# A feed-forward stage with silu moved to ScalarE and its down product in half-precision pairs

## The chip, the cores and the metric

The kernel runs on one core of one Trainium2 chip. The metric is device time in microseconds (us) of one execution; several executions are summed up by their median. Four compute engines work side by side and meet only at semaphores: TensorE (PE, matrix products; PEld is its loading of weights), VectorE (DVE), ScalarE (ACT) and GpSimd (POOL). SyncE (SP) issues the transfers. SBUF is the on-chip memory, PSUM the banks into which TensorE writes.

## The reference, cut to what matters

A block of a network over x of 8 x 256 tokens x 256 features: a modulated layer norm, a gated delta-rule attention (16 key heads, 32 value heads), a residual, and a second modulated layer norm with a sparse feed-forward. The change lies in the feed-forward:

```python
h = silu(einsum('bsh,hi->bsi', x, w_gate)) * einsum('bsh,hi->bsi', x, w_up)   # 256 -> 1024
h_sparse = sparsify_2to4(h)      # of each 4 neighbours the 2 largest in magnitude stay
y = einsum('bsi,ih->bsh', h_sparse, w_down)                                     # 1024 -> 256
x = x + gb * y                   # gb: gate of the sequence, at least 0.25 in magnitude
```

silu(g) is g * sigmoid(g), which equals g * (tanh(g / 2) + 1) / 2. Everything is asked for in float32.

## The kernel before

One program holds all the work. A long loop of 64 steps (16 heads x 4 pairs of sequences) computes the attention and takes some 1,900 us. Around 1,925 us `last_bodies` drains it, while the weights of the feed-forward are loaded and split. Then 16 units follow (`for u in range(UNITS)` on each engine), and these are what the change touches. The order of each engine's instructions is written out by hand; engines wait for one another by semaphores (`need(engine, name, count)`).

A unit u is one half (512) of the 1,024 features for a pair of token tiles, as four planes, so that the four neighbours of a group lie in four planes at the same place. It has 128 partitions x 1,024 values. The steps of a unit:

- PE: `gate(u)` and `up(u)`, 24 half-precision products each. Weights and activations are each held as a high and a low half-precision part, and three products (high x high, high x low, low x high) stand for one float32 product. `gate` writes bank 2 to 5 (two banks for even, two for odd units), `up` banks 6 and 7.
- ACT: `gate_tanh(u)`, two halves of 512, into `cc` (`f_th`, L1304); `magnitude(u)`, the absolute values of 1,024 (L1310).
- DVE: `silu(u)`, (tanh + 1) times the gate bank, two halves of 512 (L1751, into `b_le`); `hidden_product(u)`, times the up bank (L1762, into `e_b` for even and `kn` for odd units); `compare` (L1770 to L1772) and `count` (L1776 to L1782) rank the four planes; `select(u)` keeps two of four (L1793) and writes one of four float32 buffers (`o`, `osq`, `zth`, `zg`).
- PE: `down(j)`, the down product of token tile j, from the two units of its pair: float32 features times float32 weights `wd_sb` (the tile `ae`).
- DVE: `gate_down(j)` (L1800) multiplies by the sequence's gate; POOL: `add_residual(j)` (L481) adds x; SP stores the tile.

Beside this the layer norm of later token tiles runs: DVE `gated` (L1727), `hidden_normed` (L1742), `hidden_stats` (L1733, L1735); POOL `add_input` (L464), `hidden_rstd` (L470, L472), `hidden_low` (L477); PE two transposes; ACT `hidden_turned`.

DVE's order in unit u is: gate_down(u-3), gated(u+5), compare(u), silu(u+1), hidden_normed(u+4), hidden_product(u+1), count(u), hidden_stats(u+5), select(u). POOL's is: add_residual(u-3), hidden_low(u+3), add_input(u+5), hidden_rstd(u+5). PE's is: gate(u+1), up(u+1), turn_hidden(u+3), down(u-2). ACT's is: gate_tanh(u+1), hidden_turned(u+3), magnitude(u+1). The layer-norm parts end with the last tiles: from unit 12 on, DVE has none of them. On DVE the last unit is followed by gate_down(14) and gate_down(15); on PE the second halves of down(14) and down(15) stand last and wait for select(15).

Of the kernel before, what the change touches and what calls it, by code (L numbers as in the profile page):

```python
# [36 lines left out]
GUARD = 0.25  # L37
W_SCALE = 64.0
# [8 lines left out]
def adaln_deltanet_ffn(nc, x, wh, nw, wba, dtb, alog, wgate, wup, wdown, cT, wmod, out):  # L47
    with ExitStack() as ctx:  # L48
# [135 lines left out]
        f_rank_in, f_th = cc_flat[:, 0:1024], cc_flat[:, 1024:2048]  # L184
        f_gate = flat(b_le[:])
        f_h = [flat(e_b[:])[:, 0:1024], kn[:].rearrange("p r t s -> p (r t s)")]
        f_s = [o[:].rearrange("p t v d -> p (t v d)"), flat(osq[:]), flat(zth[:]), flat(zg[:])]
# [134 lines left out]
        def _(pool):  # L322
# [212 lines left out]
        def _(pe):  # L535
# [462 lines left out]
            def down_part(j, hh, first, last):  # L998
# [3 lines left out]
                need(pe, "f_s", u + 1)  # L1002
                if first:
                    pe.wait_ge(sig("wd_dma"), 16)
                    pe.wait_ge(sig("ya"), STEPS * 2)
                    need(pe, "yo_mul", j - 1 if j > NT - 4 else j)
                s_ = f_s[u % 4].rearrange("p (i n) -> p i n", i=PLANES)
# [60 lines left out]
        def _(act):  # L1068
# [229 lines left out]
            def gate_tanh(u):  # L1298
                if u == 0:
                    act.wait_ge(sig("w_lo"), NK * 4 + 8)  # L1300
                need(act, "f_silu", u * 2)
                for hf in range(2):
                    act.wait_ge(sig("gate_ps"), u * 2 + hf + 1)
                    A(f_th[:, hf * 512:hf * 512 + 512], bank[2 + u % 2 * 2 + hf][:], ACT.Tanh,  # L1304
                      scale=0.5 / W_SCALE).then_inc(sig("f_tanh"), 1)
# [76 lines left out]
            def last_bodies(s0, s1, s2, s3):  # L1382
                if not s2:
                    gate_tanh(0)
# [15 lines left out]
                if s2:  # L1400
# [16 lines left out]

        @block.vector
        def _(dve):
# [54 lines left out]
            def guard_gates():  # L1474
# [8 lines left out]
                V.tensor_scalar(gate_rows[:, 1], gate_rows[:, 1], 0.5 / (W_SCALE * W_SCALE), None, ALU.mult).then_inc(sig("gate_rows"), 1)  # L1483
# [239 lines left out]

            def gated(j):
# [20 lines left out]
            def silu(u):  # L1745
                if u == 0:
                    dve.wait_ge(sig("eb"), STEPS)
                for hf in range(2):
                    dve.wait_ge(sig("f_tanh"), u * 2 + hf + 1)
                    hs = slice(hf * 512, hf * 512 + 512)  # L1750
                    V.scalar_tensor_tensor(f_gate[:, hs], f_th[:, hs], 1.0, bank[2 + u % 2 * 2 + hf][:], ALU.add,  # L1751
                                           ALU.mult).then_inc(sig("f_silu"), 1)

            def hidden_product(u):
                need(dve, "f_abs", u - 1)
                if u == 1:
                    dve.wait_ge(sig("knt_ps"), STEPS)
                for hf in range(2):
# [3 lines left out]
                    V.tensor_tensor(f_h[u % 2][:, hs], f_gate[:, hs], bank[6 + hf][:], ALU.mult).then_inc(sig("f_h"), 1)  # L1762
# [21 lines left out]
            def select(u):  # L1784
# [91 lines left out]
            def last_bodies(s0, s1, s2, s3):  # L1876
                if not s2:
                    silu(0)
# [21 lines left out]
                if s2:  # L1900
                    gated(TL)

            all_steps(dve, body, last_bodies)
            for u in range(UNITS):
# [16 lines left out]
                select(u)  # L1921
            for j in range(UNITS - 2, UNITS):
# [53 lines left out]
```

## Time and profile before

| what | value |
|---|---|
| median of 3 runs | 2140.26 us (2139.37 to 2140.46) |
| the profiled execution, its own time | 2142.45 us |
| its span in the profile | 2140.7 us |
| PE busy | 2038.0 us (95%) |
| DVE busy | 1954.9 us (91%) |
| ACT busy | 1632.9 us (76%) |
| POOL busy | 1404.1 us (66%) |
| mean granted TensorE clock | 0.982 |

Busy times are sums over the whole program, and nearly all of it is the attention loop. The stage that is changed is the last 150 us, where the shares are others. The span leaves out 1.75 us of the execution's own time.

### The profile page before, as it was taken

To read this page: it belongs to the slowest core of one execution; us is meant where nothing else is said; L and a number is where in the kernel's file an instruction comes from. 1 tells how busy PE (TensorE), PEld (TensorE's weight loads), DVE (VectorE), ACT (ScalarE), POOL (GpSimd) and SP (SyncE) were. 2 spreads that over 40 slices of the span, in tenths; PEclk is the share of its full clock that TensorE was granted. 3 is DMA by queue.
4 is the path that set the end of the run, shared out by engine and by line. 5 is a ranking of instruction groups with operands and counts; after the bars stand their busy time and mean duration, and the time that the engine had idled before them with its cause. 6 is when DMAs were issued, how large, how long until landed. Compare 5 with 4: busy or idle time off the path is not lost. (4 is left out here: it accounts for less than half of the span.)

```text
span 2140.7 us, 61867 instructions
## 1 busy us (share of the span) xinstructions
PE 2038.0 (95%) x23974; PEld 1686.3 (79%) x23974; DVE 1954.9 (91%) x3216; ACT 1632.9 (76%) x3275; POOL 1404.1 (66%) x896
## 2 busy tenths in 40 slices
PE   5699999999999999999999999999999999998898
PEld 4377888787888888888878888888888888887787
DVE  5689999999999999999999999999999999985998
ACT  3488888888888888888888888888888887885332
POOL 3367667677667777666777666777766677763352
PEclk7799999999999999999999999999999999998999
DMA  2000000000000000000000000000000000003000
GB/s 107 4 2 22 2 22 2 22 2 22 2 22 2 12 12 2 22 2 22 2 22 2 22 2 22 2 2 22 2 22 2 22 2 21 2 9 102 6 24 22
DMA packets 12403, 34.07 MB, mean 16 GB/s; under 512 B 1100, under 2 KB 9420, under 8 KB 9684
## 3 DMA queue, kind: packets, MB, share of 16 engines
q1 hardware_dynamic: 12116, 30.11, 4.0%
q8 instruction: 196, 3.21, 0.6%
q14 instruction: 91, 0.75, 0.1%
HBM read 27.99 MB, written 2.11 MB: 14 GB/s over the span
## 5 line engine op out<-in xcount | busy, mean ns | idle before, releaser
L1567 DVE SCALAR_TENSOR_TENSOR cc<-bank,wc,cc 128x510 f32<-128x510 f32 (+2 forms) x768 | 535.0, 738 | 3.2 <-ACT cc L1118 3.0
L539 PE MATMUL bank<-h,w 128*128 128x512 f16 (+1 forms) x1920 | 421.1, 360 | 4.7 <-DVE cc L1567 2.8
L1193 ACT ACTIVATE inv<-bank 128x512 f16<-128x512 f32 x384 | 231.5, 603 | 89.4 <-PE bank L539 84.4
L415 POOL TENSOR_TENSOR e_b<-ae,b_le 128x1024 f32<-128x1024 f32 x64 | 151.8, 2372 | 214.0 <-ACT ae L1183 214.0
L539 PEld LDWEIGHTS bank<-h,w 128*128 128x128 f16 x1920 | 174.7, 98 | 136.3 <-issue 7.3
L1646 DVE TENSOR_TENSOR yl<-bank,mask 128x512 f16<-128x512 f32 x384 | 263.6, 686 | 19.7 <-PE bank L539 18.0
L1118 ACT ACTIVATE cc<-bank,wc 128x512 f32<-128x512 f32 x256 | 176.1, 688 | 127.9 <-PE bank L539 127.8
L381 POOL TENSOR_TENSOR g_le<-le,hg 128x1024 f16<-128x1024 f16 x128 | 239.9, 1897 | 25.3 <-DVE hc L1522 25.3
L1197 ACT ACTIVATE invT<-bank 128x512 f16<-128x512 f32 x384 | 234.0, 609 | 27.4 <-PE bank L539 27.4
L539 PEld LDWEIGHTS bank<-inv,a 128*128 128x128 f16 x3584 | 186.8, 98 | 59.4 <-ACT inv L1193 18.2
L539 PE MATMUL bank<-inv,a 128*128 128x64 f16 (+1 forms) x3584 | 218.7, 197 | 3.2 <-ACT inv L1193 3.2
L397 POOL TENSOR_TENSOR rn<-n2m,mhalf 128x4 f32<-128x4 f32 x64 | 64.9, 1014 | 222.9 <-DVE n2m L1583 222.9
L423 POOL TENSOR_TENSOR osq<-o,zg 128x1024 f32<-128x1024 f32 x64 | 151.6, 2369 | 81.1 <-DVE oss L1683 81.1
L539 PE MATMUL bank<-w,h 128*128 128x256 f16 x1536 | 188.9, 273 | 5.1 <-DVE y_acc L1707 4.7
L430 POOL TENSOR_TENSOR a_lo<-ae,a_hi 128x1024 f16<-128x1024 f32 x64 | 151.2, 2363 | 54.9 <-ACT a_hi L1189 54.9
L539 PE MATMUL bank<-w,goT 128*128 128x256 f16 x1536 | 179.8, 274 | 2.1 <-DVE goT L1696 2.1
L539 PE MATMUL bank<-yl,invT 128*128 128x64 f16 x3072 | 153.1, 193 | 22.7 <-DVE yl L1646 19.2
L539 PEld LDWEIGHTS bank<-w,goT 128*128 128x128 f16 x1536 | 150.9, 98 | 19.6 <-DVE goT L1696 2.3
L542 PE MATMUL bank<-ident,cc 128*128 128x128 f32 x1024 | 158.3, 277 | 0.2 <-ACT kx L1170 0.2
L539 PEld LDWEIGHTS bank<-w,h 128*128 128x128 f16 x1536 | 141.3, 98 | 21.6 <-DVE y_acc L1707 6.6
L539 PE MATMUL bank<-invT,yl 128*128 128x64 f16 x3072 | 153.0, 193 | 0.4 <-DVE yl L1646 0.4
L539 PEld LDWEIGHTS bank<-yl,invT 128*128 128x128 f16 x3072 | 129.3, 97 | 29.9 <-DVE yl L1646 23.9
(214 smaller groups left out, 5339.3 us busy)
## 6 DMA issues: line engine op xcount, KB each, us to landing
w_raw<-in_wh SPq DMA_DIRECT2D x16, 1032.0 KB, 4.8
v<-in_x SPq DMA_DIRECT2D x4, 512.0 KB, 4.0
out<-sol SPq DMA_DIRECT2D x16, 128.0 KB, 1.7
w_raw<-in_wgate SPq DMA_DIRECT2D x1, 1024.0 KB, 4.7
cc<-in_wup SPq DMA_DIRECT2D x1, 1024.0 KB, 5.0
pt<-gate_store SPq DMA_DIRECT2D x2, 512.0 KB, 4.2
ae<-in_wdown SPq DMA_DIRECT2D x1, 1024.0 KB, 6.5
sol<-gate_store SPq DMA_DIRECT2D x2, 512.0 KB, 5.7
```

The costliest lines, as they stand in the source:

```text
L381: gp.tensor_tensor(g_le[:, part], le16[:].unsqueeze(1).broadcast_to([P, U, P]), hg[:, par(s), part, ts].rearrange("p t v -> p (t v)").unsq ...
L397: gp.tensor_tensor(rn[:], n2m[:, blk(s), 0], mhalf[:, 0:TL], ALU.pow).then_inc(sig("rn"), 1)
L415: gp.tensor_tensor(e_b[:, :, 1:P + 1], e_raw, b_le[:], ALU.mult).then_inc(sig("eb"), 1)
L423: gp.tensor_tensor(flat(osq[:]), o[:].rearrange("p t v d -> p (t v d)"), flat(zg[:]), ALU.mult).then_inc(sig("zo"), 1)
L430: gp.tensor_tensor(a_lo[:, ring(s)], at, a_hi[:], ALU.subtract).then_inc(sig("al"), 1)
L539: return mm(o_, l_, r_, start=start, stop=stop, skip_group_check=True)
L542: return nc.tensor.transpose(o_, i_, id_)
L1118: A(cc[:, i], bP[i % 2][:], ACT.Copy, scale=wc[:, par(s), i, 3:4]).then_inc(sig("tap"), 1)
L1193: A(lefts(inv[:, ring(s)], l), halves(bL[0], l), ACT.Copy).then_inc(sig("x_ready"), 1)
L1197: A(rights(invT[:, ring(s)], l), halves(bL[1], l), ACT.Copy).then_inc(sig("xt_ready"), 1)
L1567: V.scalar_tensor_tensor(dst, src, wc[:, par(s), i, 3 - j:4 - j], dst, ALU.mult, ALU.add).then_inc(sig(f"conv{i}"), 1)
L1646: V.tensor_tensor(lefts(yl[:, l], l), halves(bL[0], l), left(mask[:, l + 1, :], l).unsqueeze(1).broadcast_to([P, U, HP // n_, n_]), ALU.mu ...
```

## The change

Four edits, all in the feed-forward:

1. `gate_silu(u)` on ACT evaluates silu from the gate bank in one instruction per half, where `gate_tanh(u)` was, and writes `b_le`. DVE's `silu(u)` is gone. `hidden_product(u)` becomes a form with a scalar (one more multiplication in the same instruction).
2. `selected_high(u)` on ACT copies the selected features of a unit (128x1024, float32) to half precision; `selected_low(u)` on POOL takes the difference from the float32 features, also to half precision (for the last unit DVE does that). The pairs lie in `inv`, `invT`, `a1` and `a_lo`. The float32 buffers go from four to two (`o`, `osq`).
3. `down_weights_high()` on ACT and `down_weights_low()` on DVE split the down weights once, in four pieces each, into `k16`, `q16` and `a_hi`, `hm`.
4. `down_part` issues three half-precision products for each float32 one.

```diff
+            def selected_low(u):
+                pool.wait_ge(sig("f_sh"), u + 1)
+                need(pool, "down_ps", (u // 2 - 1) * 2)
...
+                gp.tensor_tensor(f_pairs[u % 4][1], f_s[u % 2], f_pairs[u % 4][0], ALU.subtract).then_inc(sig("f_sl"), 1)
...
             for u in range(UNITS):
                 if u >= 3:
                     add_residual(u - 3)
+                if u >= 1:
+                    selected_low(u - 1)
                 if 0 < u < NT - 3:
                     hidden_low(u + 3)
...
-                need(pe, "f_s", u + 1)
+                need(pe, "f_sh", u + 1)
+                if u + 1 < UNITS:
+                    need(pe, "f_sl", u + 1)
+                else:
+                    need(pe, "f_sl_last", 1)
...
                 for p_ in range(PLANES):
-                    ins = m(bk[:, (j % 2) * C:(j % 2) * C + C], s_[:, p_, j % 2 * P:j % 2 * P + P], wd_sb[:, 2 * p_ + hh, :],
-                            start=(first and p_ == 0), stop=(last and p_ == PLANES - 1))
+                    f = 2 * p_ + hh
+                    right_ = [wd_parts[a][f // 4][:, f % 4 * C:f % 4 * C + C] for a in range(2)]
+                    for i, (a, b_) in enumerate(((0, 0), (0, 1), (1, 0))):
+                        ins = m(bk[:, (j % 2) * C:(j % 2) * C + C], left_[a][:, p_], right_[b_],
+                                start=(first and p_ == 0 and i == 0), stop=(last and p_ == PLANES - 1 and i == 2))
...
-            def gate_tanh(u):
+            def down_weights_high():
+                act.wait_ge(sig("wd_dma"), 16)
+                need(act, "kx_ps", STEPS)
+                for q in range(4):
+                    A(wd_parts[0][q // 2][:, q % 2 * 512:q % 2 * 512 + 512], wd_flat[:, q * 512:q * 512 + 512], ACT.Copy,
+                      scale=W_SCALE).then_inc(sig("w_hi"), 1)
+
+            def gate_silu(u):
...
+                need(act, "f_h", u * 2)
                 for hf in range(2):
                     act.wait_ge(sig("gate_ps"), u * 2 + hf + 1)
+                    A(f_gate[:, hf * 512:hf * 512 + 512], bank[2 + u % 2 * 2 + hf][:], ACT.Silu,
+                      scale=1.0 / W_SCALE).then_inc(sig("f_silu"), 1)
+
+            def selected_high(u):
+                act.wait_ge(sig("f_s"), u + 1)
+                need(act, "down_ps", (u // 2 - 1) * 2)
...
+                A(f_pairs[u % 4][0], f_s[u % 2], ACT.Copy).then_inc(sig("f_sh"), 1)
...
+            def down_weights_low():
+                need(dve, "tm_ps", STEPS * 2)
+                need(dve, "al", STEPS)
+                for q in range(4):
+                    dve.wait_ge(sig("w_hi"), NK * 4 + 8 + q + 1)
+                    qs_ = slice(q % 2 * 512, q % 2 * 512 + 512)
+                    V.scalar_tensor_tensor(wd_parts[1][q // 2][:, qs_], wd_flat[:, q * 512:q * 512 + 512], W_SCALE,
+                                           wd_parts[0][q // 2][:, qs_], ALU.mult, ALU.subtract).then_inc(sig("w_lo"), 1)
...
-            def silu(u):
...
-                    V.tensor_tensor(f_h[u % 2][:, hs], f_gate[:, hs], bank[6 + hf][:], ALU.mult).then_inc(sig("f_h"), 1)
+                    V.scalar_tensor_tensor(f_h[u % 2][:, hs], bank[6 + hf][:], H_SCALE / W_SCALE, f_gate[:, hs], ALU.mult,
+                                           ALU.mult).then_inc(sig("f_h"), 1)
...
                 select(u)
+            selected_low(UNITS - 1)
             for j in range(UNITS - 2, UNITS):
                 gate_down(j)
```

What stands on DVE in one full unit, before. `sol` is gate_down, `y_acc` gated, `yl<-cc` compare, `b_le<-cc,bank` silu, `w_raw` hidden_normed, `e_b` hidden_product:

```order
L1800 TENSOR_TENSOR sol<-bank,sol 128x256
L1727 SCALAR_TENSOR_TENSOR y_acc<-y_acc,pt 128x256
L1770 TENSOR_TENSOR yl<-cc 128x768
L1771 TENSOR_TENSOR yl<-cc 128x256
L1772 TENSOR_TENSOR yl<-cc 128x512
L1751 SCALAR_TENSOR_TENSOR b_le<-cc,bank 128x512 x2
L1742 TENSOR_SCALAR w_raw<-y_acc,f_small 128x256
L1762 TENSOR_TENSOR e_b<-b_le,bank 128x512 x2
```

and in the changed kernel:

```order
L1851 TENSOR_TENSOR sol<-bank,sol 128x256
L1784 SCALAR_TENSOR_TENSOR y_acc<-y_acc,pt 128x256
L1820 TENSOR_TENSOR yl<-cc 128x768
L1821 TENSOR_TENSOR yl<-cc 128x256
L1822 TENSOR_TENSOR yl<-cc 128x512
L1799 TENSOR_SCALAR w_raw<-y_acc,f_small 128x256
L1811 SCALAR_TENSOR_TENSOR e_b<-bank,b_le 128x512 x2
```

The two silu instructions are gone, and the rest of the unit keeps its order. On POOL a full unit reads, before (`sol` add_residual, `h` hidden_low, `y_acc` add_input, `f_small` hidden_rstd):

```order
L481 TENSOR_TENSOR sol<-sol,y_acc 128x256
L477 TENSOR_TENSOR h<-sq,h 128x2x128
L464 TENSOR_TENSOR y_acc<-y_acc,v 128x256
L470 TENSOR_TENSOR f_small<-f_small,eps 128x1
L472 TENSOR_TENSOR f_small<-f_small,mhalf 128x1
```

and in the changed kernel:

```order
L494 TENSOR_TENSOR sol<-sol,y_acc 128x256
L490 TENSOR_TENSOR inv<-o,inv 128x1024
L483 TENSOR_TENSOR h<-sq,h 128x2x128
L470 TENSOR_TENSOR y_acc<-y_acc,v 128x256
L476 TENSOR_TENSOR f_small<-f_small,eps 128x1
L478 TENSOR_TENSOR f_small<-f_small,mhalf 128x1
```

One instruction of 1,024 columns now stands between the residual and hidden_low. The end of DVE's program reads, in the changed kernel (before, the row of `a_lo` is not there):

```order
L1832 TENSOR_TENSOR yl<-yl 128x1024
L1844 SCALAR_TENSOR_TENSOR osq<-yl,kn 128x1024
L1779 TENSOR_TENSOR a_lo<-osq,a_lo 128x1024
L1851 TENSOR_TENSOR sol<-bank,sol 128x256 x2
```

The subtraction of the last unit stands between the last select and the last two gate_down.

## Rows read from the trace of the kernel before

**Rows 1.** Windows: us, then busy us (count) of PE, PEld, DVE, ACT, POOL, PEclk, DMA
```profile
2050.00:2100.00 50.00, 47.73 (x351) 41.30 (x349) 49.66 (x89) 16.69 (x31) 23.69 (x24) 1.00 0.07 23
```

**Rows 2.** Timeline of DVE, one unit: start us, us, what
```profile
2055.13 0.42 DVE L1800 TENSOR_TENSOR sol<-bank,sol 128x256 f32<-128x256 f32 x1
...
2055.80 0.95 DVE L1770 TENSOR_TENSOR yl<-cc 128x768 f16<-128x768 f32 x1
2056.67 0.95 DVE L1771 TENSOR_TENSOR yl<-cc 128x256 f16<-128x256 f32 x1
2057.54 1.15 DVE L1772 TENSOR_TENSOR yl<-cc 128x512 f16<-128x512 f32 x1
2058.62 1.27 DVE L1751 SCALAR_TENSOR_TENSOR b_le<-cc,bank 128x512 f32<-128x512 f32 x2
2059.81 0.40 DVE L1742 TENSOR_SCALAR w_raw<-y_acc,f_small 128x256 f32<-128x256 f32 x1
...
2064.74 0.42 DVE L1800 TENSOR_TENSOR sol<-bank,sol 128x256 f32<-128x256 f32 x1
```

**Rows 3.** Timeline of POOL in the same unit
```profile
2055.86 1.48 POOL L481 TENSOR_TENSOR sol<-sol,y_acc 128x256 f32<-128x256 f32 x1
2057.30 0.85 POOL L477 TENSOR_TENSOR h<-sq,h 128x256 f16<-128x256 f32 x1
2058.11 1.17 POOL L464 TENSOR_TENSOR y_acc<-y_acc,v 128x256 f32<-128x256 f32 x1
```

**Rows 4.** One line of code each: ns min/median/max, first and last start
```profile
L1521 DVE COPY hg<-g_cols x16: 189/2355/2358, 66.2 to 1795.3; 128x64 f16<-128x64 f16 x16
L430 POOL TENSOR_TENSOR a_lo<-ae,a_hi x64: 2127/2338/2463, 88.7 to 1919.0; 128x1024 f16<-128x1024 f32 x64
L477 POOL TENSOR_TENSOR h<-sq,h x12: 699/850/1042, 1999.3 to 2104.6; 128x256 f16<-128x256 f32 x12
```

**Rows 5.** Timeline of POOL, attention loop
```profile
1795.24 2.39 POOL L415 TENSOR_TENSOR e_b<-ae,b_le 128x1024 f32<-128x1024 f32 x1 [3.37 <-ACT ae L1183]
```

**Rows 6.** Timeline of PE in the same unit
```profile
2055.70 1.97 PE L539 MATMUL bank<-ae,o 128*128 128x256 f32 x8 [0.45 <-DVE sol L1800]
...
2059.22 2.78 PE L539 MATMUL bank<-h,w 128*128 128x256 f16 x24
2061.84 0.38 PE L539 MATMUL bank<-h,g_le 128*128 128x256 f16 x2
```

**Rows 7.** Groups from 1,880 us on: xcount | busy us, mean ns
```profile
L1304 ACT ACTIVATE cc<-bank 128x512 f32<-128x512 f32 x32 | 17.4, 587 | 1.1 <-PE bank L539 0.9
L1310 ACT ACTIVATE cc<-e_b 128x1024 f32<-128x1024 f32 x8 | 8.5, 1057 | 36.1 <-DVE e_b L1762 36.1
```

**Rows 8.** Timeline of DVE, the third compare of unit 12
```profile
2104.47 0.68 DVE L1772 TENSOR_TENSOR yl<-cc 128x512 f16<-128x512 f32 x1
```

**Rows 9.** Timeline of DVE and PE at the end
```profile
2129.77 1.97 PE L539 MATMUL bank<-ae,zth 128*128 128x256 f32 x8 [0.48 <-DVE sol L1800]
...
2131.92 1.23 DVE L1793 SCALAR_TENSOR_TENSOR zg<-yl,kn 128x1024 f32<-128x1024 f16 x1
2133.20 3.72 PE L539 MATMUL bank<-ae,zg 128*128 128x256 f32 x16 [1.46 <-DVE zg L1793]
```

**Rows 10.** Timeline of POOL and DVE in the drain
```profile
1975.71 1.48 POOL L477 TENSOR_TENSOR h<-sq,h 128x256 f16<-128x256 f32 x2
1979.16 1.90 POOL L449 TENSOR_TENSOR go<-osq,osc 128x1024 f32<-128x1024 f32 x1
1981.77 0.43 DVE L1733 BATCH_NORM_STATS2 f_small<-y_acc 128x6 f32<-128x256 f32 x1 [3.91 <-POOL y_acc L464]
```

**Rows 11.** Windows in the drain, columns as in rows 1
```profile
1982.00:1985.00 3.00, 0.95 (x10) 0.64 (x9) 2.88 (x6) 2.50 (x4) 0.74 (x2) 1.00 0.00 0
1985.00:1988.00 3.00, 3.00 (x18) 2.18 (x16) 0.69 (x1) 0.66 (x2) 0.00 (x0) 0.53 0.00 0
```

**Rows 12.** Timeline of ACT in the drain
```profile
1981.86 1.27 ACT L1265 ACTIVATE goT<-bank,nw_sb 128x512 f16<-128x512 f32 x2 [8.66 <-PE bank L542]
```

More of the change, by code:

```diff
@@ L37 @@
 GUARD = 0.25
+H_SCALE = 8.0
 W_SCALE = 64.0
@@ L183, in adaln_deltanet_ffn @@
         h_f = sq[:].rearrange("p r t s -> p (r t s)").rearrange("p (t k s) -> p t k s", k=CK, s=P)
-        f_rank_in, f_th = cc_flat[:, 0:1024], cc_flat[:, 1024:2048]
+        f_rank_in = cc_flat[:, 0:1024]
         f_gate = flat(b_le[:])
+        wd_parts = [[flat(b_) if b_.shape[1] == U else b_.rearrange("p r t s -> p (r t s)") for b_ in pair]
+                    for pair in ((k16[:], q16[:]), (a_hi[:], hm[:]))]
+        f_pairs = [[b_[:].rearrange("p r u s -> p (r u s)")[:, a * FF:a * FF + FF] for a in range(2)]
+                   for b_ in (inv, invT, a1, a_lo)]
         f_h = [flat(e_b[:])[:, 0:1024], kn[:].rearrange("p r t s -> p (r t s)")]
-        f_s = [o[:].rearrange("p t v d -> p (t v d)"), flat(osq[:]), flat(zth[:]), flat(zg[:])]
+        f_s = [o[:].rearrange("p t v d -> p (t v d)"), flat(osq[:])]
         f_adj, f_part, f_keep = (yl[:, i].rearrange("p u s -> p (u s)").rearrange("p (i n) -> p i n", i=PLANES)
@@ L1296, in hidden_turned @@
                 A(h16[:, 0, :, b, ts], h_f[:, j % 4], ACT.Copy).then_inc(sig("f_hi"), 1)
-            def gate_tanh(u):
+            wd_flat = wd_sb.rearrange("p f c -> p (f c)")
+            def down_weights_high():
[5 more added lines that the diff above has]
+            def gate_silu(u):
                 if u == 0:
                     act.wait_ge(sig("w_lo"), NK * 4 + 8)
-                need(act, "f_silu", u * 2)
+                    act.wait_ge(sig("eb"), STEPS)
+                need(act, "f_h", u * 2)
                 for hf in range(2):
                     act.wait_ge(sig("gate_ps"), u * 2 + hf + 1)
-                    A(f_th[:, hf * 512:hf * 512 + 512], bank[2 + u % 2 * 2 + hf][:], ACT.Tanh,
-                      scale=0.5 / W_SCALE).then_inc(sig("f_tanh"), 1)
+                    A(f_gate[:, hf * 512:hf * 512 + 512], bank[2 + u % 2 * 2 + hf][:], ACT.Silu,
[3 more added lines that the diff above has]
+                need(act, "down_ps", (u // 2 - 1) * 2)
+                if u == 0:
+                    act.wait_ge(sig("tm_ps"), STEPS * 2)
+                A(f_pairs[u % 4][0], f_s[u % 2], ACT.Copy).then_inc(sig("f_sh"), 1)
             def magnitude(u):
@@ L1415, in _ @@
                     magnitude(u + 1)
+                selected_high(u)
         @block.vector
@@ L1743, in hidden_normed @@
                                 ALU.subtract, ALU.mult).then_inc(sig("xn"), 1)
-            def silu(u):
[L1746 to L1752, printed above, removed]
             def hidden_product(u):
                 need(dve, "f_abs", u - 1)
+                need(dve, "f_s", u - 1)
                 if u == 1:
@@ L1877, in last_bodies @@
                 if not s2:
-                    silu(0)
                     hidden_stats(TL)
@@ L1909, in _ @@
                 compare(u)
-                if u + 1 < UNITS:
-                    silu(u + 1)
-                else:
+                if u + 1 == UNITS:
                     gate_down(u - 2)
```

24 lines of the change are left out of this document (17 added, 7 removed).

## The prediction

> **What bounds the kernel now.** I read the windows first, to see which engine limits the feed-forward, then the timelines of DVE and POOL side by side over one unit, then PE's, and last the end and the drain.
>
> In the feed-forward DVE is busy 49.66 of 50 us and PE 47.73, ACT and POOL have time [rows 1]. A unit lasts 2064.74 - 2055.13 = 9.61 us from one gate_down to the next [rows 2]. PE waits 0.45 us in it for gate_down [rows 6], so without DVE its own work would be 9.16 us. DVE sets the period; a cut on DVE alone would be worth at most 0.45 us before PE takes over, which is why the down product matters.
>
> The reader is to see a second thing, in the compare: L1771 has 256 columns and lasts 0.95 us, as long as L1770 with 768, and L1772 with 512 lasts 1.15 us [rows 2], where in unit 12, with POOL idle, it lasts 0.68 [rows 8]. The POOL rows explain it. add_residual starts at 2055.86 while L1770 runs (to 2056.75) and ends at 2057.34; L1771 ends 0.28 us after it. hidden_low follows, ends at 2058.15, and L1772 ends 0.54 us after that [rows 2, 3]. The two engines take turns: an instruction of one that reads two SBUF operands stands until the other's is done. While silu ran (L1751, one operand in PSUM), add_input ran beside it and DVE kept its 0.6 us per half [rows 2, 3]. It holds for long instructions too: a DVE copy that takes 0.19 us took 2.35 where a POOL instruction of 2.39 us had started just before [rows 4, 5]. DVE is released about 0.2 us before the end that POOL's row shows.
>
> The Trainium skill states this as a rule (SBUF — State Buffer, Who interferes with whom): a VectorE instruction with two SBUF inputs and a GpSimd one that reads SBUF exclude each other for a whole instruction, and one whose second operand is in PSUM is not touched. The trace agrees, by the 2.35 us just named. By this rule the change pays on DVE for what it puts on POOL; on the reading that idle POOL time is free the sum would be that of the first rival below.
>
> **Part by part.**
>
> *silu.* DVE loses L1751, two halves, 2059.81 - 2058.62 = 1.19 us a unit [rows 2], in the 15 units that compute the next one's. Silu itself has no row. ACT's functions over a 512-column bank take 0.587 (tanh) [rows 7]; I bound Silu between that and twice it, and take 0.59. At either end it is hidden: ACT is busy 16.69 of 50 us [rows 1], and the product needs it about 4 us into the unit, while ACT can start at some 1.3 us. One change of function table falls into ACT's idle 8.66 us of the drain [rows 12]. hidden_product keeps one operand in PSUM and, I take it, its length; L1751, which has the form that it gets, took 1.27 for two halves of the same size [rows 2], bounds 0 and 0.1.
>
> *down product.* Sixteen float32 instructions took 2059.22 - 2055.70 = 3.52 us, 24 half-precision ones take 2061.84 - 2059.22 = 2.62 [rows 6]. PE's work falls from 9.16 to 8.26 us a unit. This is gain only as far as DVE becomes faster than 9.16.
>
> *selected_high.* 1,024 columns on ACT: as L1310, 1.06 us [rows 7]. It starts when select ends, so POOL can have its result 0.1 + 1.06 + 0.1 = 1.3 us after the unit's start; with the tail of select itself, 1.35.
>
> *selected_low.* The same shape and types as L430, whose shortest is 2.13 us [rows 4]. It stands behind add_residual, which ends 2057.34 - 2055.13 = 2.21 us into a unit [rows 2, 3]; by then its operand has been there for 0.8 us. So it takes exactly the turn that hidden_low has now, between L1771 and L1772. L1772 stood for hidden_low's 0.70 us [rows 4] and now stands for 2.13: +1.43 us. hidden_low comes after L1772, beside hidden_normed (L1742, one SBUF tensor) and the product, where add_input already costs nothing.
>
> So a full unit gains 1.19 and loses 1.43: +0.24 us, 9.85. DVE stays the bound over PE's 8.26. Bounds of the turn: 0, if POOL's instruction hid entirely, and 2.13 + 0.60, if hidden_low then also held hidden_normed. I take 1.43, because the rows show this very turn.
>
> Counting the units:
> - Unit 0: silu gone, no selected_low yet: -1.2.
> - Units 1 and 2: no add_residual. Two short turns of about 1.0 us in all go, one of about 1.9 (2.13 less the early release) comes: -0.3 each, -0.6.
> - Units 3 to 10: 8 x 0.24 = +1.9; unit 11, still with hidden_low: +0.2.
> - Units 12 to 14: nothing of POOL's met L1772 here (0.68) [rows 8], so the turn costs 1.9: 3 x (1.9 - 1.19) = +2.1.
> - Unit 15: no silu was there to remove: +1.9.
>
> *The end.* select(15) is followed by PE 0.05 us later and 16 instructions of 3.72 us [rows 9]. Now come ACT's copy (1.06), DVE's subtraction (1,024 columns, as the select of 1,024: 1.2) and two more handovers of 0.1: +2.5. Then 24 half-precision instructions, 2.78 busy instead of 3.72 [rows 6, 9]: -0.9. Net +1.6. Here the cover of DVE and POOL is gone and all counts. PE also stands idle: its first half of down(15) runs before the select (as at 2129.77 [rows 9]), and then it waits for some 5 us. In the drain three microseconds with 0.95 busy were followed by a clock of 0.53, that is 1.2 GHz most of the time, in the next three [rows 11]; before the last products the idle was only 1.46 us [rows 9]. At 1.2 GHz throughout, the 24 would take 2.6 us more. I take half of that: +1.3 (bounds 0 and 2.6).
>
> *The drain.* Splitting the down weights costs DVE four instructions of 0.6 us with two SBUF operands. DVE is idle there for 3.91 us [rows 10], so their own time is hidden, but they take turns with POOL, on which the idle DVE waits: hidden_low until 1977.19, then the scale and L449 of 1.90 us, then the residual add [rows 10]. Each can be held once, by 0.6 at most. Bounds 0 and 4 x 0.6 = 2.4; I take 1.5, with the next PE work as much later. If cover is lacking altogether it is 2.4.
>
> Sum: -1.2 - 0.6 + 1.9 + 0.2 + 2.1 + 1.9 + 1.6 + 1.3 + 1.5 = +8.7 us. The profiled execution took 2142.45 us, 2.19 above the median of the runs shown, 2140.26. So 2151.2 for such an execution and 2149.0 for the median.
>
> **The rivals.**
>
> *POOL's subtraction is free.* For it: POOL is idle half the time [rows 1], and the removed silu is real. Against it: the 2.35 us copy [rows 4, 5] and the very turns of rows 2 and 3. Then the period is 9.61 - 1.19 = 8.42, just over PE's 8.26; 15 x -1.19 = -17.9, end +1.6: -16.3, 2124. Faster.
>
> *The subtraction slips behind L1772.* If ACT's copy is ready only after about 2.4 us instead of 1.35 (Silu or the copy far longer than the rows, or ACT held by another wait), L1772 goes first, POOL's 2.13 us lie beside hidden_normed and the product (0.33 + 1.19 = 1.5, not touched) and hold the count for 0.6 - 0.2. A unit then changes by -1.19 - 0.47 (L1772 no longer held) + 0.4 = -1.2; over 14 units -15 at most, less in the tail, with the end, drain and unit 15 +5: about -10, 2130. Against it: 1 us of slack in the row arithmetic.
>
> *PE's clock falls inside the units.* In even units the second half of down waits for the subtraction, until 4.4 us into the unit, and PE is idle up to 2.6 us, where it was 0.45. If the clock then drops to 1.2 GHz for 3 us, 1.5 us of work are lost. Two units on PE: 2 x 8.26 + 2.6 + 1.5 = 20.6 against DVE's 19.7: +0.9 a pair, +6 in all: 2155. Idle of this size is already there around 1980 with both outcomes, so I give it a small chance.
>
> *Nearly even.* The turn as I have it, but end and drain at their low bounds: -1.3 for the clock, -1.5 for the drain, and 1.0 instead of 1.9 for each of the last four units (POOL delayed beside the product): +2, 2142.
>
> **How the numbers follow.** Forecast 0.62; subtraction free 0.08; slips behind 0.12; clock in the units 0.10; nearly even 0.08. The likeliest case alone spans 2145 to 2154: drain 0 to 2.4, clock 0 to 2.6, and 0.15 us either way on twelve units. The range for 8 in 10 is 2137 to 2157: it leaves out the free case and most of the slipping one. A difference under 0.2% (4.3 us) can't be told from none in this kernel. Slower by more: the forecast and the clock case, 0.73; within: 0.08, faster 0.19.
>
> **What would show it.** In the changed profile: the third compare (L1822) at about 2.6 us in units 3 to 14, and L490 of POOL with 2.1 to 2.4 us just before; period 9.85 in full units, near 8.8 in units 12 to 14; PE busy about 84% in the stage; three us more between the last select and the first of the last products than before, and the clock of the last 3 us at 0.5 or 1.0. The mechanism is wrong if L1822 stays near 1.15 or 0.68 us; the order is wrong if L1826 is the one that grows.

## The result and the profile after

| | before | changed |
|---|---|---|
| median, 4 runs each | 2140.05 us (2139.37 to 2140.46) | 2153.98 us (2152.57 to 2155.08) |
| the profiled execution, its own time | 2142.45 us | 2152.57 us |
| its span | 2140.7 us | 2150.9 us |
| mean granted clock | 0.982 | 0.981 |

The change makes the kernel slower by a small but clear amount: 1.0065 times the time before [95% interval 1.0048 to 1.0083]. The forecast was 2149.0 us, in a range of 2137 to 2157. Stage by stage, in the two profiled executions:

| stretch | before | changed | difference | forecast |
|---|---|---|---|---|
| start of unit 0 (gated, L1727 and L1784) | 1989.42 | 1987.54 | -1.9 | +1.5 |
| unit 0, to the end of its select | 8.87 | 7.69 | -1.2 | -1.2 |
| units 1 and 2 | 18.52 | 18.71 | +0.2 | -0.6 |
| units 3 to 10 | 76.82 | 81.92 | +5.1 | +1.9 |
| unit 11 | 8.85 | 9.48 | +0.6 | +0.2 |
| units 12 to 14 | 24.15 | 26.33 | +2.2 | +2.1 |
| unit 15 | 6.52 | 8.45 | +1.9 | +1.9 |
| last select to the last gate_down | 4.23 | 7.39 | +3.2 | +2.9 |
| sum | | | +10.1 | +8.7 |

Units are counted from the end of one select to the next. Of the -1.9 in the first line, -1.1 is there already at the last subtraction of the attention loop (L430 starts at 1918.97 before, L436 at 1917.84 in the changed kernel), where the two programs do not differ yet. The windows of the changed kernel, columns as in [rows 1]:

```profile
2050.00:2100.00 50.00, 42.33 (x381) 36.77 (x380) 49.66 (x74) 21.00 (x35) 34.74 (x31) 1.00 0.06 18
```

DVE is as full as before, with 74 instructions in place of 89. PE fell from 47.73 to 42.33 us and POOL rose from 23.69 to 34.74. The work that left DVE did not free it: an instruction that is held counts as busy all the while. Its timeline shows why; this unit answers to [rows 2]:

```profile
2054.81 0.42 DVE L1851 TENSOR_TENSOR sol<-bank,sol 128x256 f32<-128x256 f32 x1
...
2056.35 0.95 DVE L1821 TENSOR_TENSOR yl<-cc 128x256 f16<-128x256 f32 x1
2057.22 2.61 DVE L1822 TENSOR_TENSOR yl<-cc 128x512 f16<-128x512 f32 x1
2059.76 0.75 DVE L1799 TENSOR_SCALAR w_raw<-y_acc,f_small 128x256 f32<-128x256 f32 x1
2060.43 1.27 DVE L1811 SCALAR_TENSOR_TENSOR e_b<-bank,b_le 128x512 f32<-128x512 f32 x2
...
2065.06 0.42 DVE L1851 TENSOR_TENSOR sol<-bank,sol 128x256 f32<-128x256 f32 x1
```

and POOL in the same unit, answering to [rows 3]:

```profile
2055.54 1.48 POOL L494 TENSOR_TENSOR sol<-sol,y_acc 128x256 f32<-128x256 f32 x1
2056.98 2.31 POOL L490 TENSOR_TENSOR a<-o,a 128x1024 f16<-128x1024 f32 x1
2059.25 1.11 POOL L483 TENSOR_TENSOR h<-sq,h 128x256 f16<-128x256 f32 x1
2060.32 0.77 POOL L470 TENSOR_TENSOR y_acc<-y_acc,v 128x256 f32<-128x256 f32 x1
```

The reader is to see three things. The third compare went from 1.15 to 2.61 us, and it ends 0.54 us after the row of POOL's subtraction, just as it ended 0.54 us after hidden_low before. hidden_normed went from 0.40 to 0.75 us, because hidden_low, pushed back by 2 us, now lies beside it. hidden_product, with an operand in PSUM, lies beside add_input (L470) and keeps its length. The period is 2065.06 - 2054.81 = 10.25 us, where it was 9.61.

PE has slack now: busy 42.33 of 50 us, 85% where the forecast named about 84%. In this unit it waits 0.41 us for the product of DVE and 0.84 for gate_down; in the unit before it waited 2.58 us for the subtraction. The 24 half-precision instructions of down take 2058.57 - 2055.95 = 2.62 us, as [rows 6] let expect:

```profile
2055.95 0.27 PE L554 MATMUL bank<-k,inv 128*128 128x256 f16 x1
...
2058.57 2.78 PE L554 MATMUL bank<-h,w 128*128 128x256 f16 x24
2061.76 0.39 PE L554 MATMUL bank<-h,g_le 128*128 128x256 f16 x2 [0.41 <-DVE e_b L1811]
```

The end, DVE first and then ACT and PE, answers to [rows 9]:

```profile
2138.89 1.23 DVE L1844 SCALAR_TENSOR_TENSOR osq<-yl,kn 128x1024 f32<-128x1024 f16 x1
2141.23 1.22 DVE L1779 TENSOR_TENSOR a_lo<-osq,a_lo 128x1024 f16<-128x1024 f32 x1 [1.12 <-ACT a_lo L1344]
2145.20 0.42 DVE L1851 TENSOR_TENSOR sol<-bank,sol 128x256 f32<-128x256 f32 x1 [2.74 <-PE bank L554]
2147.09 0.42 DVE L1851 TENSOR_TENSOR sol<-bank,sol 128x256 f32<-128x256 f32 x1 [1.46 <-PE bank L554]
```
```profile
2140.14 1.06 ACT L1344 ACTIVATE a_lo<-osq 128x1024 f16<-128x1024 f32 x1 [7.38 <-DVE osq L1844]
```
```profile
2142.60 0.27 PE L554 MATMUL bank<-k,a_lo 128*128 128x256 f16 x1 [2.34 <-DVE a_lo L1779]
```

Copy and subtraction put 2142.60 - 2140.12 = 2.48 us between the select and PE (forecast: 2.5 more than the 0.05 of before). Then the granted clock of the 24 products is 0.62, mostly its lower level of 1.2 GHz:

```profile
2142.60:2147.10 4.50, 4.45 (x24) 3.12 (x24) 0.44 (x2) 0.00 (x0) 0.72 (x1) 0.62 0.00 0
```

In the drain the splits of the weights on DVE are held by POOL, and no cost of that is seen. Columns as in [rows 10]:

```profile
1976.93 1.29 DVE L1773 SCALAR_TENSOR_TENSOR a_hi<-ae,k 128x512 f16<-128x512 f32 x2
1978.14 3.52 DVE L1773 SCALAR_TENSOR_TENSOR hm<-ae,q 128x512 f16<-128x512 f32 x2
1981.58 0.41 DVE L1790 BATCH_NORM_STATS2 f_small<-y_acc 128x6 f32<-128x256 f32 x1
```
```profile
1978.06 1.91 POOL L455 TENSOR_TENSOR go<-osq,osc 128x1024 f32<-128x1024 f32 x1
1979.93 1.17 POOL L470 TENSOR_TENSOR y_acc<-y_acc,v 128x256 f32<-128x256 f32 x1
```

Two pieces that take 1.29 us alone took 3.52 beside POOL, but they end where DVE had stood idle anyway: L1790 starts at 1981.58, where L1733 had started at 1981.77. What did change there is the clock. The 24 products on `goT` took 4.46 us before and 2.79 after, the first and the second of these lines:

```profile
1984.31 4.46 PE L539 MATMUL bank<-w,goT 128*128 128x256 f16 x24 [2.05 <-DVE goT L1696]
```
```profile
1984.11 2.79 PE L554 MATMUL bank<-w,goT 128*128 128x256 f16 x24 [2.04 <-DVE goT L1737]
```

This is a difference between two executions rather than between two kernels, as a second profiled execution of the changed kernel shows (e11).

### The profile page after: what moved, and what is told of

Same layout as the page of the kernel before. It is cut to its first block, busy times and chain, and to the rows that moved or that the text cites. A ratio compares the mean times of both kernels' runs of the same rounds, so it can differ in the third digit from the quotient of the medians.

```text
span 2150.9 us, 62192 instructions
## 1 busy us (share of the span) xinstructions
PE 2026.5 (94%) x24102; PEld 1677.0 (78%) x24102; DVE 1967.0 (91%) x3189; ACT 1649.5 (77%) x3296; POOL 1438.1 (67%) x911
## 4 chain that ended last, share of the span: by engine, by line
PE 82%; DVE 11%; issue 5%; ACT 1%; POOL 1%; DMA 0%; DVEq 0%; SPq 0%; POOLq 0%; ACTq 0%
PE bank L554 73%; PE bank L557 9%; DVE yl L1822 1%; DVE oss L1724 1%; DVE yl L1687 1%; DVE yl L1820 1%; DVE w L1633 0%; DVE k L1644 0%; DVE yl L1826 0%; DVE y_acc L1748 0%; DVE kn L1811 0%; DVE e_b L1811 0%; DVE y_acc L1784 0%; DMA cc<-in_wmod 0%; DVE cc L1608 0%
## 5 line engine op out<-in xcount | busy, mean ns | idle before, releaser
L436 POOL TENSOR_TENSOR a_lo<-ae,a_hi 128x1024 f16<-128x1024 f32 x64 | 151.0, 2359 | 56.4 <-ACT a_hi L1211 56.4
```

What stands on the lines that cost most here:

```text
L436: gp.tensor_tensor(a_lo[:, ring(s)], at, a_hi[:], ALU.subtract).then_inc(sig("al"), 1)
```

## The experiments

Theory A is that of the forecast: POOL's subtraction and DVE's instructions with two SBUF operands take turns, so DVE pays for POOL's 2.3 us. The rival B: PE, or the chain select, copy, subtraction, down, gate_down, has become longer, and DVE waits at its end. The rival C: the clock falls inside the units. Each ratio is to the kernel before, run on the same chip, with its 95% interval.

**e1_low_on_dve.** The subtraction of each unit moves from POOL to DVE, behind compare.

```diff
-                if u >= 1:                  # POOL
-                    selected_low(u - 1)
...
                 compare(u)                  # DVE
+                if u >= 1:
+                    selected_low(u - 1, "f_sl")
```

> The changed kernel with the subtraction of the selected features on DVE in all units (behind compare) instead of POOL. Theory (POOL's subtraction and DVE's two-SBUF-operand instructions exclude each other): DVE loses the 1.46 us stand of L1822 and the 0.35 us stand of hidden_normed and gains an instruction of 1.13 us start to start, so a full unit lasts 9.5 to 9.6 us instead of 10.24, and the whole is about 2143 us (2140 to 2147). Rival (PE's wait for the pairs in the even units sets the period): the pairs are ready no earlier, so it stays at 2151 to 2155.

Measured: 2140.51 us (10 runs), 1.0015 [1.0003, 1.0027]; period 9.45 us in full units, 7.99 in units 12 to 14. DVE got an instruction more and each unit became 0.8 us shorter:

```profile
2044.34 0.68 DVE L1822 TENSOR_TENSOR yl<-cc 128x512 f16<-128x512 f32 x1
2044.94 1.21 DVE L1779 TENSOR_TENSOR invT<-osq,invT 128x1024 f16<-128x1024 f32 x1
2046.08 0.75 DVE L1799 TENSOR_SCALAR w_raw<-y_acc,f_small 128x256 f32<-128x256 f32 x1
```

The work itself is 1.21 us on DVE; being held for it cost 2.61 - 0.68 = 1.93. A is confirmed and B falls: PE starts on the pairs 4.37 us after the unit's gate_down (2046.30 - 2041.93) where it was 4.60 in the changed kernel (2049.18 - 2044.58), and that gain of 0.23 can't give 0.8. One expected term did not come: hidden_normed stays at 0.75 us, since hidden_low still lies beside it. The period follows without it, 10.24 - 1.93 + 1.14 = 9.45, with 1.14 from the start of the new instruction to the start of the next.

**e2_low_left_out.** No low part of the features for units 0 to 15; `down` goes on reading the buffers (this leaves a part of the computation out).

```diff
-                if u >= 1:
-                    selected_low(u - 1)
...
-                if u + 1 < UNITS:
-                    need(pe, "f_sl", u + 1)
...
-            selected_low(UNITS - 1)
```

> The changed kernel without computing the low parts of the selected features (stale numbers take their place in the products; 24 products per tile stay). Theory (exclusion): L1822 returns to about 1.15 us, hidden_normed to 0.40, a full unit lasts 8.4 to 8.5 us, just over PE's 8.26, and the whole takes about 2127 us (2124 to 2132). Rival (something else in the change, the copy on ACT or PE's finer waits, carries the loss): over 2140 us.

Measured: 2124.79 us (4 runs), 0.9938 [0.9917, 0.996]. This is about what the change would be worth if the subtraction were free. PE, with as many products as in the changed kernel, is never idle in the windows row, at a period of 8.08 us:

```profile
2050.00:2100.00 50.00, 50.00 (x461) 44.94 (x459) 49.09 (x85) 26.47 (x42) 21.42 (x23) 1.00 0.06 20
```

So PE was no bound of the changed kernel, whose period is 10.24. The expected period of 8.4 to 8.5 was DVE's, with a third compare still held to 1.15 us; measured was PE's own, 5.24 + 0.22 + 2.62 = 8.08. The compare (L1816) takes 0.68, because hidden_low now waits for ACT and comes after it, beside the product:

```profile
2062.32 0.67 POOL L483 TENSOR_TENSOR h<-sq,h 128x256 f16<-128x256 f32 x1 [1.24 <-ACT h L1312]
```

**e8_low_zeroed.** POOL fills the low part with zeros instead of subtracting (the low part of the features is left out for units 0 to 14; for the last one DVE subtracts as before).

```diff
-                gp.tensor_tensor(f_pairs[u % 4][1], f_s[u % 2], f_pairs[u % 4][0], ALU.subtract).then_inc(sig("f_sl"), 1)
+                gp.memset(f_pairs[u % 4][1], 0.0).then_inc(sig("f_sl"), 1)
```

> The changed kernel with POOL filling the low parts with zeros (an instruction that reads nothing) in place of the subtraction, so the low parts of the selected features are left out. Theory with the exclusion of reads alone: DVE's compare does not stand for it, L1822 is at 0.68 to 1.1 us, PE binds at 8.1 us a unit, near 2125 us (2121 to 2130). Rival (any POOL instruction on SBUF shuts DVE out): L1822 stands for as long as the fill lasts (0.5 to 1 us for 1,024 half-precision columns), a unit 8.4 to 9.0.

Measured: 2125.11 us (4 runs), 0.993 [0.9909, 0.9951], period 8.08. POOL has an instruction at the same place, and the compare beside it isn't held. Here are POOL and DVE:

```profile
2063.76 0.95 POOL L490 MEMSET inv<- 128x1024 f16 x1
```
```profile
2064.02 0.68 DVE L1822 TENSOR_TENSOR yl<-cc 128x512 f16<-128x512 f32 x1
```

It is POOL's reading of SBUF that excludes DVE, not its being busy there. The Trainium skill says this on the page SBUF — State Buffer, Who interferes with whom: a GpSimd instruction that only writes doesn't contend with a VectorE one that has two SBUF inputs. The trace agrees, with 0.68 us. So engines do not meet only at semaphores, as the introduction has it: GpSimd and VectorE also meet at SBUF.

**e7_half_subtraction.** POOL subtracts 512 of the 1,024 columns (half of the low part is left out for units 0 to 14).

```diff
-                gp.tensor_tensor(f_pairs[u % 4][1], f_s[u % 2], f_pairs[u % 4][0], ALU.subtract)...
+                gp.tensor_tensor(f_pairs[u % 4][1][:, 0:512], f_s[u % 2][:, 0:512], f_pairs[u % 4][0][:, 0:512], ALU.subtract)...
```

> The changed kernel with POOL computing the low parts of the first 512 of 1,024 columns only (the other half stays stale). Theory (DVE stands for as long as POOL's instruction lasts): L490 falls from 2.13 to about 1.07 us, L1822 from 2.61 to about 1.55, a full unit from 10.24 to 9.2, and the 14 units with it give back 15 us: 2139 us (2136 to 2142). Rival (a fixed price per turn, not its length): L1822 stays above 2.3 and the time above 2150.

Measured: 2138.20 us (10 runs), 0.9994 [0.998, 1.0008]; period 9.27. POOL's row and the compare's:

```profile
2061.85 1.33 POOL L490 TENSOR_TENSOR a_lo<-osq,a_lo 128x512 f16<-128x512 f32 x1
```
```profile
2062.09 1.64 DVE L1823 TENSOR_TENSOR yl<-cc 128x512 f16<-128x512 f32 x1
```

With before and after this makes a series: rows of POOL of 0.85, 1.33 and 2.31 us hold the compare for 1.15, 1.64 and 2.61 less its own 0.68, that is 0.47, 0.96 and 1.93 us. Each hold is POOL's row less 0.38. In all three POOL's row starts 0.24 us before the compare's and ends 0.54 or 0.55 before the compare's end; for an instruction that starts at another moment within POOL's, the hold is not measured.

**e3_silu_alone.** Silu on ACT, the down product in float32 as before; nothing is left out.

```diff
-                    A(f_th[...], bank[2 + u % 2 * 2 + hf][:], ACT.Tanh, scale=0.5 / W_SCALE)...
+                    A(f_gate[...], bank[2 + u % 2 * 2 + hf][:], ACT.Silu, scale=1.0 / W_SCALE)...
...
-                if u + 1 < UNITS:           # DVE
-                    silu(u + 1)
```

> The kernel before with only silu moved to ScalarE; the down product stays float32. Theory: DVE's unit would be 8.42 us, PE's own 9.16 binds, so a full unit lasts about 9.2 us and the last ones 8.7; PE's work from unit 1 to the end (14 x 5.24 for gate and up, 16 x 3.45 for down, 12 x 0.4 for transposes, about 134 us from 1991) ends near 2126, so about 2131 us (2128 to 2136). Rival (Silu on ScalarE is slow or its wait binds DVE): at 2140 or above.

Measured: 2133.99 us (10 runs), 0.9977 [0.9966, 0.9988]: faster than both kernels by a little more than the 0.2% that the prediction took as the least that can be told, and the best of those that compute everything. Period 8.92, all of it PE's:

```profile
2050.00:2100.00 50.00, 50.00 (x368) 44.09 (x367) 48.82 (x81) 19.98 (x35) 23.58 (x24) 1.00 0.05 16
```

PE's float32 down takes 2053.10 - 2049.65 = 3.45 us here without a wait, where I had 3.52 from [rows 6]:

```profile
2049.65 1.89 PE L540 MATMUL bank<-ae,o 128*128 128x256 f32 x8
...
2053.10 2.78 PE L540 MATMUL bank<-h,w 128*128 128x256 f16 x24
```

**e5_down_alone.** The other half of the change: down in pairs, silu still with tanh and DVE's product.

```diff
-                    A(f_gate[...], bank[2 + u % 2 * 2 + hf][:], ACT.Silu, scale=1.0 / W_SCALE)...
+                    A(f_th[...], bank[2 + u % 2 * 2 + hf][:], ACT.Tanh, scale=0.5 / W_SCALE)...
...
+                if u + 1 < UNITS:           # DVE
+                    silu(u + 1)
```

> The changed kernel with tanh on ScalarE and the silu product back on DVE: the half-precision down product alone, without the silu edit. Theory (exclusion, terms add up): L1822 still stands for POOL's subtraction; the silu instructions come back with 1.19 us in 15 units, and POOL's hidden_low runs beside them, so that hidden_normed no longer stands: 10.24 + 1.19 - 0.35 = 11.08 us a full unit, 9.97 in units 12 to 14; in all 14 us above the changed kernel, near 2167 us (2163 to 2171). Rival (gains and losses of the two edits are not additive, since PE or the pair chain binds): below 2160.

Measured: 2171.36 us (4 runs), 1.0146 [1.0121, 1.017], 4 us over the value expected (near 2167) and just outside its range (2163 to 2171); period 11.08, as expected. Its units 1 to 15 are 12.9 us longer than the changed kernel's and unit 0 has 1.2 more, the 14 us of the sum; what is over lies outside them (in its profile select(0) ends at 2003.69 us). The turn is there in full, and hidden_normed, now behind silu, keeps its 0.40 us:

```profile
2059.70 2.60 DVE L1830 TENSOR_TENSOR yl<-cc 128x512 f16<-128x512 f32 x1
2062.22 1.27 DVE L1807 SCALAR_TENSOR_TENSOR b_le<-cc,bank 128x512 f32<-128x512 f32 x2
2063.41 0.40 DVE L1798 TENSOR_SCALAR w_raw<-y_acc,f_small 128x256 f32<-128x256 f32 x1
```

The two halves of the change are of opposite sign: per full unit silu alone gives 9.60 - 8.92 = 0.68 us and is then stopped by PE, and the pairs cost 11.08 - 9.60 = 1.48.

**e4_normed_behind_product.** hidden_normed and hidden_product change places on DVE, so that the product lies beside hidden_low.

```diff
-                if u + 4 < NT:
-                    hidden_normed(u + 4)
                 if u + 1 < UNITS:
                     hidden_product(u + 1)
+                if u + 4 < NT:
+                    hidden_normed(u + 4)
```

> The changed kernel with DVE's hidden_normed issued behind hidden_product instead of ahead of it. Theory: hidden_normed (0.75 us where it was 0.40) stands for POOL's hidden_low; behind the product, whose second operand is in PSUM, it no longer does, so L1799 returns to 0.40 us and 11 units gain 0.35 each: about 2150 us (2148 to 2152). Rival (the stand moves on, to add_input's turn): L1799 stays near 0.75 and the time at 2153 to 2155.

Measured: 2154.22 us (4 runs), 1.007 [1.005, 1.0089]. The mechanism is as expected: hidden_normed is back at 0.40 and the period is 9.89, 0.35 less; the 15 units after the first take 141.08 us instead of 144.89.

```profile
2061.96 2.61 DVE L1822 TENSOR_TENSOR yl<-cc 128x512 f16<-128x512 f32 x1
2064.50 1.28 DVE L1811 SCALAR_TENSOR_TENSOR e_b<-bank,b_le 128x512 f32<-128x512 f32 x2
2065.70 0.40 DVE L1799 TENSOR_SCALAR w_raw<-y_acc,f_small 128x256 f32<-128x256 f32 x1
```

The time was missed: the median didn't move. In its profiled execution select(0) ends at 2002.04 us, 6.8 later than in the changed kernel's, and the clock around unit 0 is at the lower level. Of the 6.8 us, 1.9 are there at the last subtraction of the loop (L436 at 1919.77 against 1917.84), and 4.9 come in the drain. The first line is e4's, the second the changed kernel's:

```profile
1987.50:1994.30 6.80, 5.90 (x29) 4.24 (x30) 2.75 (x5) 2.03 (x3) 0.00 (x0) 0.51 0.00 0
```
```profile
1987.50:1994.30 6.80, 6.80 (x65) 6.08 (x63) 6.73 (x15) 1.06 (x1) 1.49 (x2) 1.00 0.01 2
```

All four runs of e4 have a mean granted clock of 0.976 or 0.977, and nine of the ten of the changed program (the first four and e11) have 0.978 to 0.981. So the lower clock may go with e4's order of instructions rather than with one execution; no run here decides it, and why the median kept still is open.

**e9_high_alone.** select writes half precision directly and down has two products where there were three; ACT's copy and POOL's subtraction are gone (the low part is left out). This takes the whole burden of the pairs away, the copy too.

```diff
-                selected_high(u)            # ACT
...
-                    for i, (a, b_) in enumerate(((0, 0), (0, 1), (1, 0))):
+                    for i, (a, b_) in enumerate(((0, 0), (0, 1))):
```

> The changed kernel with select writing half precision itself, so that neither ScalarE's copy nor any subtraction is there, and two products (features x high and x low weights) instead of three. The low parts of the selected features are left out: the down product sees them in half precision. Theory: PE's unit is 5.24 + 0.22 + 1.75 = 7.2 us, DVE's about 8.0 (7.4 of its own and one turn of add_residual), so DVE binds at 8.0 us; the end loses the copy, the last subtraction and 8 products, about 3 us; near 2121 us (2117 to 2125). Rival (the DVE form with half-precision output is slower, or the select waits for PE): above 2126.

Measured: 2125.99 us (6 runs), 0.9945 [0.9928, 0.9961], outside what I expected. The period is 8.82 us, longer than e2's 8.08, though there is less to do. The half-precision output isn't the reason: select takes 1.21 us, as in e2. Without the subtraction and with a shorter unit of PE, POOL's short instructions meet DVE again; DVE, then POOL:

```profile
2055.96 1.15 DVE L1815 TENSOR_TENSOR yl<-cc 128x512 f16<-128x512 f32 x1
2057.03 0.81 DVE L1792 TENSOR_SCALAR w_raw<-y_acc,f_small 128x256 f32<-128x256 f32 x1
```
```profile
2055.72 0.85 POOL L483 TENSOR_TENSOR h<-sq,h 128x256 f16<-128x256 f32 x1
2056.52 1.17 POOL L470 TENSOR_TENSOR y_acc<-y_acc,v 128x256 f32<-128x256 f32 x1
```

These two holds, 1.15 - 0.68 and 0.81 - 0.40, are 0.88 us, and the period is 0.82 over the 8.0 expected. I had counted them as gone. That the operand of hidden_low decides where it falls is my reading: POOL waits 1.24 us for it in e2 and not at all in e9.

**e6_filler and e10_filler_20.** Is the slow end the clock, and is PE's wait its cause? While PE waits for the last subtraction, it computes products that nobody reads: 36 of them in e6, 20 in e10.

```diff
+                if hh == 1:
+                    pe.wait_ge(sig("f_h"), UNITS * 2)
+                    for _ in range(36):     # 20 in e10
+                        m(bank[6][:, 0:C], h16[:, 0, 0, 0, 0:P], h16[:, 0, 0, 0, 0:C])
```

> The changed kernel with 36 products more on PE (their results are not used) in the wait between the first and the second halves of the last two down products. Theory (PE's clock has fallen by the time the last 24 products run): the clock at the end stays at 2.4 GHz, and the time from the last select to the last gate_down falls from 7.4 us to 5.5, in all 1 to 2 us below the changed kernel, 2151 to 2153. Rival (the clock has no part in it; it is the copy, the subtraction and the hand-overs alone): 7.4 us stay.

> The changed kernel with 20 more products on PE in the last wait, where 36 lasted 1.4 us longer than the wait and gave back what the clock gained. Theory: 20 end in time, the last 24 products run at 2.4 GHz in 2.6 us, and from the last select to the last gate_down it takes 5.5 to 5.8 us instead of 7.4; the time is 1 to 2 us under the changed kernel's. Rival (20 are too few to keep the clock up): 7.4 us stay.

Measured: e6 2154.28 us (4 runs), 1.0067 [1.0046, 1.0087]; e10 2152.19 us (4 runs), 1.006 [1.0044, 1.0075]. In both the last 24 products run at full clock, in about 2.6 us instead of 4.3. In e6 the fill was too long and ended 1.4 us after the subtraction was ready: 7.16 us from the last select to the last gate_down, against 7.39. The fill of e10 is in place:

```profile
2140.43 2.35 PE L554 MATMUL bank<-h 128*128 128x256 f16 x20
2142.94 0.27 PE L554 MATMUL bank<-k,a_lo 128*128 128x256 f16 x1 [0.16 <-DVE a_lo L1783]
```
```profile
2144.45 0.42 DVE L1855 TENSOR_TENSOR sol<-bank,sol 128x256 f32<-128x256 f32 x1 [1.65 <-PE bank L554]
2145.76 0.42 DVE L1855 TENSOR_TENSOR sol<-bank,sol 128x256 f32<-128x256 f32 x1 [0.89 <-PE bank L554]
```

It has 5.73 us from the last select to the last gate_down, 1.66 less. Taken alone this would show that the wait brings the low clock. e11, below, takes that reading away: it has the same 5.73 us with no fill at all, and so have e1, e4, e5 and e8. The medians, 1.8 us lower with e10 and none with e6, are at the limit of what can be told.

**e11_changed_again.** The changed kernel once more, on the chip that ran e9 and e10.

> The changed kernel itself once more, to have it beside the others on one chip and to see how its stages vary. Both theories: 2152 to 2155 us, full unit 10.24 us, units 12 to 14 8.78 us; if the time before the first select varies between executions by a few us with TensorE's clock, this profile shows another value there than 1995.2.

Measured: 2154.60 us (6 runs), 1.0073 [1.0059, 1.0087]. Its profiled execution took 2159.18 us, 6.6 more than the first one, of the same program. Its full units have the same 10.24 us, although the clock fell in several of them, here for 3.4 us:

```profile
2036.60:2040.00 3.40, 3.17 (x16) 2.27 (x17) 3.40 (x7) 0.81 (x1) 1.89 (x3) 0.52 0.02 5
```

C thus happens, and costs nothing, since a unit of 10.24 us leaves PE 2.16 us over its own 8.08. What differs lies ahead of the units: select(0) ends at 2003.32 us, not 1995.23. Of these 8.1 us, 3.2 are there at the last subtraction of the loop (L436 at 1921.07 against 1917.84), and 4.9 come in the drain, with the clock at its lower level from 1988.8 to 1995.6:

```profile
1988.80:1995.60 6.80, 5.91 (x29) 4.25 (x30) 2.75 (x5) 2.03 (x3) 0.00 (x0) 0.51 0.00 0
```

At the end it is the other way round. Over the 24 products ahead of the last select the clock is at its lower level for the most part in both executions, and so it is over the last 24 in the first one; here these have the full one.

```profile
2150.70:2153.50 2.80, 2.73 (x24) 2.27 (x24) 0.43 (x1) 0.00 (x0) 0.72 (x1) 1.00 0.00 0
```

The last gate_down comes 5.73 us after the last select, instead of 7.39 in the first execution of the same program. So 1.66 us of the end are the clock, and 5.73 - 4.23 = 1.50 are the longer chain. PE's wait ahead of them was 1.54 us here and 2.34 in the first execution; but in e8, after a wait of 3.46 us, they ran at full clock too, and in e2, after 3.05 us, mostly at the lower one. The row of e8:

```profile
2116.50:2119.20 2.70, 2.70 (x24) 2.25 (x24) 0.43 (x1) 0.00 (x0) 0.68 (x1) 1.00 0.02 6
```

So the wait just ahead of the products does not decide their clock, and the rise with e10's fill is not shown to be the fill's doing.

## Why the prediction was right, point by point

- **The turn.** Forecast +1.43 us per full unit; measured 2.61 - 1.15 = 1.46. e1, e7 and e8 show the mechanism, not only the size: on DVE the work costs 1.21, half the length costs half, and a POOL instruction that reads nothing costs nothing. The rival "POOL's subtraction is free" would have given 2124; e2 and e8 come near that case, at 2124.79 and 2125.11 (with a period of 8.08 us and not its 8.42, so the closeness is in part luck).
- **Silu.** 1.19 us of DVE went per unit. ACT's Silu takes 1.06 us for two halves as tanh did, and hidden_product kept its 1.27 us. Its table load of 1.28 us fell into idle time of ACT.
- **hidden_normed, the term that I missed.** I had it as the upper bound of the turn and set it to nothing, since I took hidden_low to lie beside an instruction with one SBUF tensor that isn't touched, "where add_input already costs nothing"; but add_input lay beside silu, which has an operand in PSUM. hidden_normed is touched: +0.35 us, and e4 takes it away again. -1.19 + 1.46 + 0.35 = +0.62, measured +0.64. Over units 1 to 11 this makes 3.9 of the 4.4 us by which the forecast of these units was short. The rows of before could have warned me. hidden_normed itself never lay beside one of POOL's there ([rows 2, 3]: it starts at 2059.81, POOL ended at 2059.28), but the copy held for 2.35 us [rows 4, 5] has a single tensor input, in SBUF. I had used it as an instance of the rule on two SBUF operands, which it is not. The Trainium skill (SBUF — State Buffer, Who interferes with whom) names copy and tensor_scalar among the VectorE operations that can take both ports and so contend. The 2.35 and the 0.75 us agree with it.
- **Tail.** Units 12 to 14 forecast +2.1, measured +2.2; unit 15 +1.9 both ways.
- **The end.** Forecast +1.6 and +1.3; measured 1.50 for the chain and 1.66 for the clock, told apart by the two executions of the changed program. Nine profiled executions end with these instructions, and the clock's part is there in two: the first of the changed kernel and e7 (7.30 us from the last select). That 1.3 came near 1.66 is luck: I had taken half of the bound as a certain cost.
- **The drain.** Forecast +1.5; not seen. The splits are held for 3.52 - 1.29 = 2.23 us, within DVE's idle 3.91 [rows 10]. In the nine profiled executions whose programs are the changed one up to there (e4 in another order of two instructions in unit 0, e2 without a wait), select(0) ended between 1994.99 and 2003.32 us. Counted from the last subtraction of the loop it took 76.6 to 82.3 us. Before took 79.3, or 78.1 less the 1.2 us more work in its unit 0. A term of 1.5 can't be read from single profiles that spread over almost 6.
- **Sum and median.** The profiles differ by 10.1 us, the medians by 13.9. Before's profiled execution lay 2.4 us above its median, the changed one's 1.4 us below. The forecast took the first offset for both. That the profiles' 10.1 lies so near the forecast's 8.7 is in part luck: units 1 to 11 were 4.4 us short, and the start of unit 0 was 3.4 too late. (By the chances of its own cases "slower" should have had 0.72 and "faster" 0.20, not 0.73 and 0.19.)
- **PE.** Its own unit is 8.08 us instead of 8.26; of no effect here, but it is the bound that e2 meets.

What stays open: why the clock of the drain differs between executions of one program, and how much of the difference of the medians it holds. That difference is 13.9 us, and 15.9 with e11 and the runs of before beside it (2154.60 and 2138.71). The units give 10.0 us, unit 0 -1.2 and the end 1.5 to 3.2: 10.3 to 12.0 us; the other 2 to 6 are within reach of the clock, but no run assigns them. Open too is what sets the clock at the end.

## What to carry to other kernels

Work moved to GpSimd isn't off VectorE's path as long as both read SBUF: ask which VectorE instruction will stand while it runs, and price the move at GpSimd's length less 0.4 us (measured where it starts just ahead of the VectorE instruction), not at VectorE's own for the same work (here 1.93 against 1.21). An instruction put into an engine's row also pushes the next one onto a new neighbour, so look at what each later instruction now lies beside. Where a change has two halves, time them apart: here one gave 0.2% and the other took 1.5%.

## What the runs showed of the hardware that was not expected

- The length of the hold follows POOL's instruction in a straight line: 0.47, 0.96 and 1.93 us for 0.85, 1.33 and 2.31 us. A fill of 1,024 half-precision columns by POOL takes 0.95 us and holds nothing.
- A float32 tensor_scalar of 256 columns with one SBUF tensor takes 0.40 us alone, nearly as long as a tensor_tensor of that size with one operand in PSUM (gate_down, 0.42), and is still held (0.75, 0.81).
- The hold goes the other way as well: hidden_low takes 1.11 us on POOL between two held instructions of DVE, 0.85 before, and 0.67 in e2, where it lies beside the product.
- The granted clock isn't the same at the same place of the same program: 0.62 or 1.00 over the last 24 products, 1.00 or 0.51 around unit 0. Profiles of one program differ by 4.9 us in the drain and by 3.2 ahead of it; one profile per kernel would have put these down to a change of code.
